# Block 3's gate projections made ahead in plain fp32, three instead of five traces multiplied on GpSimd, and the two lanes of blocks 1 to 7 side by side

## The chip, the cores and the metric

The kernel runs on one core of one Trainium2 chip. The metric is the device time of one execution in microseconds (us), and a run's time is a little longer than the span of its profile, which goes from the first to the last instruction. Engines are called as in the profile: PE is TensorE, DVE VectorE, ACT ScalarE, POOL GpSimd, SP SyncE (here it only issues DMAs).

## What is computed

The input x is 16 sequences of 256 positions with 256 features. Four layers follow one another, each added to its input; the middle two need the whole of what came before, so nothing of a token's layer 3 can start before its layers 1 and 2 are done.

```
ctx      = scan(x, tau_ctx)                                  # h = alpha*h + x_t along the sequence
wg       = sigmoid([x, ctx] @ Wg.T + bg);  gated = x * wg    # the gate projection
mod      = 0.5 + sigmoid(gelu(x @ Wn1.T + bn1) @ Wn2.T + bn2)
temporal = sum_d softmax(blend)_d * scan(gated * mod_d, tau_d)   # 16 traces, d = 0..15
out      = (gelu(x @ Wsoma.T + bsoma) * sigmoid(temporal @ Wtemp.T + btemp)) @ Wout.T
x = x + layernorm(out) * gamma + beta                        # layer 1
x = x + masked attention pooling of x (tanh, exp, one mask of three per sequence)   # layer 2
x = x + (1-sg) * sum_e g_e * (silu(x@Wg_e) * (x@Wu_e)) @ Wd_e + sg * (the same with shared weights)  # layer 3, 8+1 experts
x = x + [gelu(x@W1+b1) @ W2, gelu(x@W1+b1) @ We[index]]      # layer 4
```

## The kernel before, in words

The 16 sequences are 8 blocks (b) of two sequences; the sequences of a block are its lanes (s = 0, 1). Layers 1 and 2 are the side work, cut into 47 pieces for each lane, j = 0 to 46. Layers 3 and 4 are 640 steps: a step takes one chunk of 128 hidden columns of one expert (or of the head, layer 4) for one block.

Of one step, `front` makes the gate and up products on PE, `late` splits the activated product, and `back`, three steps later, makes the down product. PE works with products of three: each fp32 operand is split into a high part of reduced precision (ACT copies) and the rest (DVE subtracts, or POOL for the hidden values), and PE adds low·high, high·low and high·high (`exact_sum`, L641 to L647). `plain_sum` (L634 to L638) multiplies in fp32 unsplit. DVE also multiplies up by the activated gate (`hid`, L1563), and `front(i)` on PE waits for `hid` of step i-2. Chunks of weights come in by SP (`w_raw`, three buffers, L546), are copied high by ACT (L1160) and low by DVE (`w_lo`, L1528); SP fetches the next one when `w_lo` of an earlier one is done.

A side piece of blocks 1 to 7 is: j = 0 the context's scan on DVE (L1303) and the high part of x on ACT, 1 and 2 the high and low halves of x and ctx, 5 the gate projection on PE (`project`, 24 matmuls), 6 gated, 7 to 22 the 16 traces (DVE multiplies and scans, POOL adds, ACT prepares the factor in `mix`), 24 a gather by POOL, 25 to 27 the split of temporal and its projection (`tgate`), 28 to 32 the output projection, 33 to 36 the layer norm (33 a matmul, 34 a reciprocal on DVE that waits for ACT's square root), 38 to 46 the attention.

All engines run the same list of work, written by `order()`. Its first part is block 0's side work alone, the prologue (LEADS, TRACES, TAILS): no step can run before it, and between its pieces stand `pre` parts, unsplit matmuls into `ps_out` that make the soma and the modulation of blocks 1 to 7 ahead, each copied out by ACT, stored to DRAM by SP and read back at block b's piece 2. Each engine keeps the order of the list, so a wait holds up everything behind it on that engine. From there on each step gets as many side pieces as a credit allows (costs in `side_cost`, budget in `step_budget`). Which lane's piece comes next is decided by the cost each has had; LAG gives lane 1 a handicap of 12 cost units, so lane 0 runs some pieces ahead. In the prologue lane 1's multiplications of traces 4, 6, 8, 10 and 12 are done by POOL (`multiply`, L1709) and lane 0's all by DVE (L1403).

Of the kernel before, what the change touches and what calls it, by code (L numbers as in the profile page):

```python
# [43 lines left out]
LAG = 12.0  # L44
# [8 lines left out]
PARTS = [(u, k) for u in range(NPRE) for k in range(3 + u % 2)]  # L53

# [15 lines left out]
HAND = [2, 2, 2, 1]  # L70
# [26 lines left out]
def side_cost(b, j):  # L97

    if 7 <= j < 7 + ND:
        return 2.1  # L100
    return {0: 1.3, 5: 1.0, 34: 1.7, 36: 1.4, 40: 1.4, 42: 1.5, 24: 0.0, 25: 0.0, 29: 0.0, 37: 0.0, 43: 0.0}.get(j, 0.7)
# [11 lines left out]
ON_PE = {2, 3, 4, 5, 27, 31, 33, 38, 40, 41, 44, 46} | set(range(7, 7 + ND))  # L113


def order():
# [8 lines left out]
    for x in LEADS + TRACES + TAILS:  # L125
        if x[0] in (0, 1):
            s, j = x
            out.append(("side", 0, s, j))
            if j < 7 + ND and (s, j) in TRACES + TAILS:
                for _ in range(HAND[slots % len(HAND)]):  # L130
                    if parts:
                        out.append(("pre", *parts.pop(0)))
                slots += 1
            elif s == 0 and 9 <= j < 12:
                out.append(("pre", *parts.pop(0)))
        else:
            out.append(x)
# [143 lines left out]
ON_POOL = (4, 6, 8, 10, 12)  # L281
# [6 lines left out]
           ["gate", "tgate", "proj", "var", "attn", "score", "xT", "probT", "pooled"])  # L288
SIDE_ACT = ((["alpha", "h1", "mod", "mod_hi", "gate0", "gate", "soma", "tgate", "sq", "cen", "std", "attn", "exp", "xT", "probT"],
             ["h1", "mod", "mod_up", "gate", "soma"] + MIXED + ["tgate0", "tgate", "sq0", "sq", "cen", "std", "attn", "exp", "xT", "probT"]),  # L290
            ["x_hi", "ctx_hi", "gate", "alpha"] + MIXED
            + ["t_hi", "tgate", "p_hi", "sq", "cen", "q_hi", "std", "attn", "exp", "xT", "probT"])
# [5 lines left out]
            + ["t_lo", "prod", "p_lo", "q_lo", "rstd", "norm", "affine", "x1", "w_hi", "w_lo", "score",  # L298
               "max", "top", "xT_lo", "den", "rden", "prob", "probT_lo", "res"])
# [3 lines left out]
SIDE_POOL = ((ADDED[:6] + ["xb"] + ADDED[6:], SECOND), ADDED + ["qsum"])  # L303


def stages_in(stages, s, b):

    return stages[1] if b else stages[0][s]
# [14 lines left out]
def residual_stack_kernel(nc, xT, chunks, head_chunks, sidew, vec128, w64, penalties, ident, we_rows,  # L323
# [6 lines left out]
    with ctx:  # L330
# [40 lines left out]
        def row_slot(s, i):  # L371
            if i == 0:
# [15 lines left out]
                   for i in range(2)]  # L388
        pre_soma = [nc.alloc_sbuf_tensor_at(f"pre_soma{i}", [P, DH * S], fp32, offset=at_)
# [89 lines left out]
        s_wide = sem("n1_wide_in")  # L479
        s_back = [sem(f"pre_back{s}") for s in range(BB)]  # L480
# [50 lines left out]
        def _(sp):  # L531
# [53 lines left out]

            load_x(0, 0)
# [17 lines left out]
            for x in ORDER:  # L604
# [28 lines left out]
        def _(pe):  # L633
# [178 lines left out]
            def side(b, s, j):  # L812
# [6 lines left out]
                if j == 5:  # L819
# [49 lines left out]

            def front(i):  # L870
                e, b, c, n = STEPS[i]
                k, slot = n % WSLOTS, b % 2
                if i == 0:
                    pe.wait_ge(pre_act, 2 * NPRE)
# [78 lines left out]
        def _(act):  # L953
# [131 lines left out]
            def side(b, s, j):  # L1085
# [3 lines left out]
                ps, both = ps_side[s], ps_both[s]  # L1089
                if j == 0:  # L1090
# [6 lines left out]
                elif j == 5:  # L1097
                    act.wait_ge(l_pe[s], pe_at(s, b, "gate"))
                    for h in range(DH):
                        last = activate(gated[s][:, h, :], both[:, h, :], ACT.Tanh, bias=half128[:, h:h + 1], scale=0.5)  # L1100
# [116 lines left out]

            def late(i):
# [38 lines left out]
        def _(dve):  # L1257
# [186 lines left out]
            def side(b, s, j):  # L1444
# [9 lines left out]
                if j == 0:  # L1454
# [10 lines left out]
                elif j == 6:  # L1465
                    dve.wait_ge(l_act[s], act_at(s, b, "gate"))
# [368 lines left out]
```

## Time and profile before

| | us |
|---|---|
| median of 3 runs (lowest, highest) | 2795.62 (2795.40, 2796.21) |
| the profiled execution | 2793.71 |
| its span | 2791.1 |
| PE busy in it | 2751.5 (99%) |
| DVE, ACT, POOL busy | 1795.5 (64%), 1450.1 (52%), 1234.8 (44%) |

A timeline row gives start, duration, engine, line, operation, output and inputs, shape, a count where equal neighbours are merged, and in brackets how long the engine was idle before it and what ended that. A plain fp32 matmul stands as two records, so x8 there is four matmuls of the code. Matmuls are pipelined: their pitch is read from starts, not from durations.

### The profile page before, as it was taken

The numbers are of one execution on the slowest core, as the hardware profiler recorded it, in microseconds if no ns is written. First come the engines' busy times: TensorE is split into PE (matmuls) and PEld (weight loads), VectorE is DVE, ScalarE is ACT, GpSimd is POOL, SyncE is SP. The second block draws the span as 40 slices with busy tenths as digits, with TensorE's granted clock in tenths as the row PEclk, the third lists the DMA queues.
The fourth block names the chain that finished last, engine by engine and source line by source line (L and its number), as shares of the span: only waits on it lengthen the run. The fifth ranks groups of instructions, "written<-read, shape, count | busy, mean of one in ns | idle before, by whom it ended". The sixth has DMA issues, their size and how long they took to land.

```text
span 2791.1 us, 36643 instructions
## 1 busy us (share of the span) xinstructions
PE 2751.5 (99%) x12730; PEld 2290.2 (82%) x12730; DVE 1795.5 (64%) x2994; ACT 1450.1 (52%) x2640; POOL 1234.8 (44%) x978
## 2 busy tenths in 40 slices
PE   7899999999999999999999999999999999999999
PEld 6678888888878888888888888888888888888888
DVE  8798778777876666557756766556765563333443
ACT  4655656565447544555545644454644463333445
POOL 7266435533654355434544445433454433333334
PEclk9999999999999999999999999999999999999999
DMA  5344333433223322122322332211321131111232
GB/s 184 108 139 123 98 108 115 132 96 107 80 61 107 94 68 68 55 61 78 98 63 57 90 92 74 59 52 57 109 84 57 43 103 46 46 46 46 80 89 59
DMA packets 119896, 232.68 MB, mean 83 GB/s; under 512 B 13849, under 2 KB 61473, under 8 KB 119713
## 3 DMA queue, kind: packets, MB, share of 16 engines
q1 hardware_dynamic: 84432, 192.46, 22.9%
q10 hardware_dynamic: 32688, 29.47, 4.6%
q0 software_dynamic: 2592, 8.41, 0.9%
q8 instruction: 102, 1.67, 0.3%
q14 instruction: 82, 0.66, 0.1%
HBM read 222.18 MB, written 8.11 MB: 83 GB/s over the span
## 4 chain that ended last, share of the span: by engine, by line
PE 93%; DVE 3%; ACT 1%; issue 1%; SPq 1%; DMA 1%; POOL 0%; ACTq 0%; DVEq 0%; POOLq 0%
PE bank L645 20%; PE bank L646 20%; PE bank L647 20%; PE ps_out L645 10%; PE ps_out L647 10%; PE ps_out L646 10%; PE bank L638 1%; DVE trace L1303 1%; DVE w_lo L1528 1%; DVE trace L1403 1%; DMA mod_rows<-stat 0%; PE bank L683 0%; SPq L550 0%; DVE hid L1563 0%; DVE trace L1477 0%
## 5 line engine op out<-in xcount | busy, mean ns | idle before, releaser
L1728 POOL TENSOR_TENSOR hid_lo<-hid,hid_hi 128x512 fp32r<-128x512 f32 x640 | 854.5, 1335 | 1485.0 <-ACT hid_hi L1231 1484.8
L645 PE MATMUL bank<-res_lo,w_hi 128*128 128x512 f32 x2428 | 952.4, 392 | 5.7 <-DVE hid L1563 4.0
L646 PE MATMUL bank<-res_hi,w_lo 128*128 128x512 f32 x2428 | 946.5, 390 | 0.0
L647 PE MATMUL bank<-res_hi,w_hi 128*128 128x512 f32 x2428 | 944.9, 389 | 0.0
L1563 DVE TENSOR_TENSOR hid<-hid,bank 128x512 f32<-128x512 f32 x576 | 394.1, 684 | 601.1 <-PE bank L647 570.9
L1199 ACT ACTIVATE hid<-bank 128x512 f32<-128x512 f32 x576 | 344.2, 597 | 587.4 <-PE bank L647 584.6
L1528 DVE TENSOR_TENSOR w_lo<-w_raw,w_hi 128x768 fp32r<-128x768 f32 (+2 forms) x520 | 496.7, 957 | 190.1 <-ACT w_hi L1160 142.1
L1160 ACT ACTIVATE w_hi<-w_raw 128x768 fp32r<-128x768 f32 x392 | 331.3, 845 | 489.6 <-PE ps_out L647 472.4
L645 PEld LDWEIGHTS bank<-res_lo,w_hi 128*128 128x128 f32 x2428 | 456.1, 188 | 98.5 <-DVE w_lo L1528 6.1
L647 PEld LDWEIGHTS bank<-res_hi,w_hi 128*128 128x128 f32 x2428 | 455.8, 188 | 96.8
L646 PEld LDWEIGHTS bank<-res_hi,w_lo 128*128 128x128 f32 x2428 | 456.2, 188 | 88.5
L645 PE MATMUL ps_out<-hid_lo,w_hi 128*128 128x512 f32 (+1 forms) x1344 | 509.7, 379 | 2.2 <-DVE acc L1586 2.0
L647 PE MATMUL ps_out<-hid_hi,w_hi 128*128 128x512 f32 (+1 forms) x1344 | 509.7, 379 | 0.0
L646 PE MATMUL ps_out<-hid_hi,w_lo 128*128 128x512 f32 (+1 forms) x1344 | 509.3, 379 | 0.0
L1231 ACT ACTIVATE hid_hi<-hid 128x512 fp32r<-128x512 f32 x640 | 398.8, 623 | 14.6 <-DVE hid L1563 13.8
L1696 POOL TENSOR_TENSOR temporal<-temporal,trace 128x512 f32<-128x512 f32 x239 | 324.3, 1358 | 11.6 <-DVE trace L1303 11.2
L1303 DVE TENSOR_TENSOR_SCAN trace<-bank,trace 128x256 f32<-128x256 f32 x480 | 304.3, 676 | 10.8 <-POOL trace L1709 2.8
L645 PEld LDWEIGHTS ps_out<-hid_lo,w_hi 128*128 128x128 f32 x1344 | 252.5, 188 | 54.9 <-issue 3.2
L646 PEld LDWEIGHTS ps_out<-hid_hi,w_lo 128*128 128x128 f32 x1344 | 252.5, 188 | 49.3
L647 PEld LDWEIGHTS ps_out<-hid_hi,w_hi 128*128 128x128 f32 x1344 | 252.5, 188 | 47.5
L1477 DVE SCALAR_TENSOR_TENSOR trace<-gated,bl,bank 128x256 f32<-128x256 f32 x448 | 193.2, 472 | 0.2 <-ACT bank L1151 0.2
L1586 DVE SCALAR_TENSOR_TENSOR acc<-ps_out,coef,acc 128x256 f32<-128x256 f32 x288 | 119.3, 476 | 1.8 <-issue 1.8
(238 smaller groups left out, 1592.1 us busy)
## 6 DMA issues: line engine op xcount, KB each, us to landing
w_raw<-in_chunks SPq DMA_DIRECT2D x392, 384.0 KB
mod_on<-mod_rows ACTq DMA_DIRECT2D x154, 128.0 KB, 3.2
w_raw<-in_head_chunks SPq DMA_DIRECT2D x64, 224.0 KB
stat<-mod_rows ACTq DMA_DIRECT2D x70, 128.0 KB
x_in<-in_xT SPq DMA_DIRECT2D x16, 256.0 KB, 3.7
pre_x<-in_xT SPq DMA_DIRECT2D x14, 256.0 KB, 7.0
soma_rows<-pre_soma SPq DMA_DIRECT2D x14, 256.0 KB
soma<-soma_rows SPq DMA_DIRECT2D x14, 256.0 KB, 4.0
```

The costliest lines, as they stand in the source:

```text
L645: mm(out, wh, xl, start=start and i == 0, stop=False, skip_group_check=not lone)
L646: mm(out, wl, xh, start=False, stop=False, skip_group_check=not lone)
L647: last = mm(out, wh, xh, start=False, stop=end, skip_group_check=not lone)
L1160: last = activate(w_hi[k][:], raw[:], ACT.Copy)
L1199: activate(h[:], ps_gate[i % 2][:], ACT.Silu).then_inc(s_act, 1)
L1231: activate(hid_hi[i % DEPTH][:], hid[i % 3][:], ACT.Copy).then_inc(s_hhi, 1)
L1303: return V.tensor_tensor_scan(out, decay.broadcast_to([P, S]), x, 0.0, ALU.mult, ALU.add)
L1477: last = STT(tr[:, h, :], gated[s][:, h, :], bl[:, h, d:d + 1], ps[:, 0:S], ALU.mult, ALU.mult)
L1528: return TT(w_lo[k][:, cols], src, f(w_hi[k][:, cols]), ALU.subtract)
L1563: TT(h[:], h[:], ps_up[i % 2][:], ALU.mult).then_inc(s_hid, 1)
L1696: nc.gpsimd.tensor_tensor(temporal[s][:], temporal[s][:], trace[s][d % 3][:], ALU.add).then_inc(l_pool[s], 1)
L1728: nc.gpsimd.tensor_tensor(hid_lo[i % DEPTH][:], hid[i % 3][:], f(hid_hi[i % DEPTH][:]), ALU.subtract).then_inc(s_hlo, 1)
```

## The change

Four things are changed. (1) Block 3's gate projections leave its side work. They are eight parts (`gate_part`), in the prologue behind the last `pre` part: for each lane x times the x half of Wg, and x times the ctx half, both unsplit. ACT copies each result out, SP stores it, and at block 3's piece 0 SP loads both into `ema` and `temporal`; at piece 2 DVE scans the one and adds the other, which gives the same as projecting the scanned x. Pieces 0, 1 and 5 of block 3 lose the rest of their work. (2) ON_POOL keeps traces 4, 6, 8; traces 10 and 12 of lane 1 are multiplied by DVE in the prologue. (3) HAND: two `pre` or gate parts behind every slot instead of 2, 2, 2, 1. (4) LAG is 0, and in one step no two tail pieces with matmuls (j over 26) may have the same j.

```diff
-LAG = 12.0
+LAG = 0.0
+AHEAD = 3
+GATES = [((AHEAD - 1) * BB + s, k0) for s in range(BB) for k0 in (0, DH)]
+PARTS += [("gate", n, h) for n in range(len(GATES)) for h in range(DH)]
-HAND = [2, 2, 2, 1]
+HAND = [2]
-ON_POOL = (4, 6, 8, 10, 12)
+ON_POOL = (4, 6, 8)
@@ order()
-                touched = set()
+                touched, tails = set(), set()
...
-                    if lane in touched and (j in ON_PE or j == 25):
+                    if lane in touched and (j in ON_PE or j == 25) or j in tails:
                         break
+                    if j > 26 and j in ON_PE:
+                        tails.add(j)
@@ SP
+            def gate_store(n, h):
+                if h == DH - 1:
+                    sp.wait_ge(gate_act, n + 1)
+                    for i in range(DH):
+                        sp.dma_start(gate_rows[n, :, i, :], gate_out[n % 2][i][:]).then_inc(s_gstore[n % 2], 16)
+            def gate_back(s):
+                sp.wait_ge(l_dve[s], dve_at(s, AHEAD - 1, "res"))
+                for i in range(2):
+                    sp.wait_ge(s_gstore[i], 16 * DH * len(GATES) // 2)
+                sp.dma_start(ema[s][:], gate_rows[BB * s + 1]).then_inc(s_gback[s], 16)
+                sp.dma_start(temporal[s][:], gate_rows[BB * s]).then_inc(s_gback[s], 16)
@@ PE
-                if j == 5:
+                if j == 5 and b == AHEAD:
+                    return
+                elif j == 5:
+            def gate_part(n, h):
+                u, k0 = GATES[n]
+                if n == 0 and h == 0:
+                    pe.wait_ge(pre_act, pre_at(NPRE - 1, "h1"))
+                elif h == 0:
+                    pe.wait_ge(gate_act, n)
+                last = plain_sum(ps_out[:, 1, h * S:(h + 1) * S], plain(wg, h, pre_x[u % len(pre_x)], k0))
+                if h == DH - 1:
+                    last.then_inc(gate_pe, 1)
@@ ACT
+            def gate_part(n, h):
+                if h < DH - 1:
+                    return
+                act.wait_ge(gate_pe, n + 1)
+                if n >= 2:
+                    act.wait_ge(s_gstore[n % 2], 16 * DH * (n // 2))
+                for i in range(DH):
+                    last = activate(gate_out[n % 2][i][:], ps_out[:, 1, i * S:(i + 1) * S], ACT.Copy)
+                last.then_inc(gate_act, 1)
@@ DVE side
+                if b == AHEAD and j < 3:
+                    if j == 2:
+                        dve.wait_ge(s_gback[s], 32)
+                        for h in range(DH):
+                            last = scan(cen[:, h, :], alpha[:, ND:ND + 1], cen[:, h, :])
+                        last.then_inc(l_dve[s], 1)
+                        mine("ctx")
+                        TT(cen[:], cen[:], temporal[s][:], ALU.add).then_inc(l_dve[s], 1)
```

The first place is PE late in the prologue, from lane 0's `tgate` (bank4<-temporal0) to lane 1's (bank5 and bank1<-temporal1). Before:

```order
77 L638 MATMUL bank4<-temporal0,acc1 128x256 x4
78 L638 MATMUL ps_out<-pre_x2_53,acc1 128x256 x2
79 L638 MATMUL ps_out<-pre_x3_54,n1_wide0_61 128x256
80 L638 MATMUL ps_out<-pre_x3_54,n1_wide1_62 128x256
81 L638 MATMUL ps_out<-pre_x3_54,acc1 128x256 x2
82 L638 MATMUL bank4<-trace0_0,acc2 128x256 x4
83 L638 MATMUL ps_out<-pre_x3_54,acc1 128x256 x2
84 L868 MATMUL bank3<-pre_small0_70,c64 128x256
85 L638 MATMUL bank0<-gated0,mean_w 128x256 x2
86 L950 MATMUL ps_out<-onehot,hid2 128x16
87 L638 MATMUL bank5<-temporal1,acc1 128x256 x2
```

After, on the same engine at the same place:

```order
83 L684 MATMUL bank4<-temporal0,acc1 128x256 x4
84 L684 MATMUL ps_out<-pre_x4_55,acc0 128x256 x8
85 L684 MATMUL bank4<-trace0_0,acc2 128x256 x4
86 L684 MATMUL ps_out<-pre_x5_56,acc0 128x256 x4
87 L684 MATMUL bank0<-gated0,mean_w 128x256 x2
88 L1012 MATMUL ps_out<-onehot,hid2 128x16
89 L684 MATMUL ps_out<-pre_x5_56,acc0 128x256 x4
90 L684 MATMUL bank5<-temporal1,acc1 128x256 x2
```

The soma and modulation parts that stood here have moved ahead of the first row, and the 16 gate matmuls (inputs pre_x4, pre_x5, weights acc0) stand in their place: eight before lane 0's output projection, four before its variance, four before lane 1's `tgate`.

The second place is DVE at the start of block 3. acc1<-bank5,temporal1 is the last piece of block 2's lane 1. Before, block 3's lane 0 had begun earlier and lane 1 starts here:

```order
652 L1520 TENSOR_TENSOR acc1<-bank5,temporal1 128x2x256
653 L1528 TENSOR_TENSOR w_lo1<-w_raw1,w_hi1 128x768
654 L1554 TENSOR_TENSOR res_lo0<-acc1,res_hi0 128x1024
655 L1563 TENSOR_TENSOR hid2<-hid2,bank3 128x512
656 L1303 SCALAR_TENSOR_TENSOR ema1<-alpha,x_in1_1 128x256 x2
657 L1477 SCALAR_TENSOR_TENSOR trace0_1<-gated0,bl,bank4 128x256 x2
658 L1303 SCALAR_TENSOR_TENSOR trace0_1<-bank4,trace0_1 128x256 x2
659 L1528 TENSOR_TENSOR w_lo2<-w_raw2,w_hi2 128x768
660 L1563 TENSOR_TENSOR hid0<-hid0,bank2 128x512
```

After:

```order
644 L1614 TENSOR_TENSOR acc1<-bank5,temporal1 128x2x256
645 L1622 TENSOR_TENSOR w_lo2<-w_raw2,w_hi2 128x768
646 L1648 TENSOR_TENSOR res_lo0<-acc1,res_hi0 128x1024
647 L1657 TENSOR_TENSOR hid0<-hid0,bank2 128x512
648 L1387 SCALAR_TENSOR_TENSOR ema0<-alpha,ema0 128x256 x2
649 L1545 TENSOR_TENSOR ema0<-ema0,temporal0 128x512
650 L1387 SCALAR_TENSOR_TENSOR ema1<-alpha,ema1 128x256 x2
651 L1545 TENSOR_TENSOR ema1<-ema1,temporal1 128x512
652 L1622 TENSOR_TENSOR w_lo3<-w_raw0,w_hi3 128x768
653 L1657 TENSOR_TENSOR hid1<-hid1,bank3 128x512
```

Both lanes now start in one step, rows 648 and 650 wait for the loads of `gate_rows`, and behind them stand a `w_lo` and the next step's `hid`. On SP the two lanes' loads, with block 4's loads of x between them, stand behind a `w_raw` that waits for row 645.

The third place is ACT at the high part of block 1's temporal in lane 1 (one_hi1<-temporal1), the input of that lane's `tgate`. Before:

```order
332 L1231 ACTIVATE hid_hi1<-hid1 128x512
333 L1160 ACTIVATE w_hi8<-w_raw2 128x768
334 L1006 ACT_TABLE_LOAD
335 L1006 ACTIVATE trace0_1,den0<-trace0_0,top0 128x256 x2
336 L1010 ACTIVATE one_hi0<-bank4 128x512
337 L1136 DMA mod_on1_0<-mod_rows 128x256
338 L1136 DMA mod_on1_1<-mod_rows 128x256
339 L1110 ACTIVATE one_hi1<-temporal1 128x512
340 L1199 ACT_TABLE_LOAD
```

After:

```order
326 L1313 ACTIVATE hid_hi0<-hid0 128x512
327 L1231 ACTIVATE w_hi7<-w_raw1 128x768
328 L1204 DMA mod_on1_0<-mod_rows 128x256
329 L1204 DMA mod_on1_1<-mod_rows 128x256
330 L1178 ACTIVATE one_hi1<-temporal1 128x512
331 L1182 ACTIVATE trace0_0<-bank4,half128 128x256 x2
332 L1270 ACTIVATE hid2<-bank1 128x512
```

Lane 0's exponentials with their table load stood before that copy; now lane 0 is at its own `tgate` there and its exponentials come many steps later.

## Rows read from the trace of the kernel before

**Rows 1.** The page: span, and busy time of each engine.
```profile
span 2791.1 us, 36643 instructions
PE 2751.5 (99%) x12730; PEld 2290.2 (82%) x12730; DVE 1795.5 (64%) x2994; ACT 1450.1 (52%) x2640; POOL 1234.8 (44%) x978
```
**Rows 2.** Stretches: PE, PEld, DVE, ACT, POOL busy, clock, DMA share, GB/s.
```profile
0.00:70.00 70.00, 55.56 (x239) 43.30 (x240) 60.71 (x129) 30.78 (x76) 49.36 (x75) 1.00 0.57 183
70.00:140.00 70.00, 59.73 (x261) 46.94 (x260) 52.78 (x89) 43.41 (x84) 19.62 (x17) 0.95 0.37 110
...
1200.00:1400.00 200.00, 200.00 (x938) 167.59 (x937) 138.97 (x240) 104.51 (x200) 92.32 (x71) 1.00 0.29 84
```
**Rows 3.** Timeline, PE: one gate projection, then two steps' first matmuls.
```profile
160.38 0.39 PE L645 MATMUL bank<-one_lo,side_hi 128*128 128x256 f32 x1 [0.54 <-DVE two_lo L1464]
...
163.32 0.40 PE L645 MATMUL bank<-res_lo,w_hi 128*128 128x512 f32 x1
...
171.51 0.39 PE L645 MATMUL bank<-res_lo,w_hi 128*128 128x512 f32 x1
...
175.59 0.39 PE L645 MATMUL bank<-res_lo,w_hi 128*128 128x512 f32 x1
```
**Rows 4.** Timeline, PE, in the prologue.
```profile
70.76 1.96 PE L638 MATMUL bank<-temporal,acc 128*128 128x256 f32 x8 [0.31 <-issue]
...
77.21 1.99 PE L638 MATMUL bank<-trace,acc 128*128 128x256 f32 x8 [1.39 <-DVE trace L1411]
...
83.40 1.96 PE L638 MATMUL bank<-temporal,acc 128*128 128x256 f32 x8 [1.20 <-DVE trace L1403]
85.20 1.89 PE L638 MATMUL bank<-trace,acc 128*128 128x256 f32 x8
...
101.42 5.66 PE L638 MATMUL bank<-soma,gated 128*128 128x256 f32 x16
```
**Rows 5.** Timeline, DVE, in the prologue.
```profile
70.39 0.84 DVE L1403 SCALAR_TENSOR_TENSOR trace<-gated,bl,bank 128x256 f32<-128x256 f32 x2
...
75.30 1.27 DVE L1303 TENSOR_TENSOR_SCAN trace<-bank,trace 128x256 f32<-128x256 f32 x2 [2.76 <-POOL trace L1709]
...
82.24 0.23 DVE L1300 TENSOR_SCALAR bias_b<-ps_out,v 128x16 f32<-128x16 f32 x1 [0.93 <-PE ps_out L950]
```
**Rows 6.** Timeline, POOL, in the prologue: lane 1's trace 12.
```profile
73.87 1.40 POOL L1709 TENSOR_TENSOR trace<-gated,weighed 128x256 f32<-128x256 f32 x2
```
**Rows 7.** Timelines of ACT, PE and DVE around waits of PE.
```profile
318.39 0.62 ACT L1110 ACTIVATE one_hi<-temporal 128x512 fp32r<-128x512 f32 x1
...
319.79 0.39 PE L645 MATMUL bank<-one_lo,side_hi 128*128 128x256 f32 x1 [0.57 <-DVE one_lo L1485]
...
820.78 1.75 DVE L1498 RECIPROCAL stat<-stat 128x256 f32<-128x256 f32 x1 [3.33 <-ACT stat L1129]
...
827.16 0.50 PE L645 MATMUL bank<-res_lo,w_hi 128*128 128x512 f32 x1 [0.73 <-DVE hid L1563]
...
833.44 1.13 PE L638 MATMUL bank<-temporal,wa 128*128 128x256 f32 x4 [1.91 <-DVE temporal L1508]
```
**Rows 8.** DMA issues: name, count, KB each, median us from issue to landing.
```profile
x_in<-in_xT SPq DMA_DIRECT2D x16, 256.0 KB, 3.7
pre_x<-in_xT SPq DMA_DIRECT2D x14, 256.0 KB, 7.0
```
**Rows 9.** Timeline, DVE, where block 2 ends and lane 1 of block 3 starts.
```profile
677.99 0.95 DVE L1528 TENSOR_TENSOR w_lo<-w_raw,w_hi 128x768 fp32r<-128x768 f32 x1
...
680.39 0.68 DVE L1563 TENSOR_TENSOR hid<-hid,bank 128x512 f32<-128x512 f32 x1
680.99 3.08 DVE L1303 TENSOR_TENSOR_SCAN ema<-alpha,x_in 128x256 f32<-128x256 f32 x2
```
**Rows 10.** Timelines of DVE and POOL beside POOL's gathers.
```profile
145.45 3.65 DVE L1528 TENSOR_TENSOR w_lo<-w_raw,w_hi 128x768 fp32r<-128x768 f32 x1
...
146.97 1.31 POOL L1728 TENSOR_TENSOR hid_lo<-hid,hid_hi 128x512 fp32r<-128x512 f32 x1
```

More of the change, by code:

```diff
@@ L113, with part @@
 ON_PE = {2, 3, 4, 5, 27, 31, 33, 38, 40, 41, 44, 46} | set(range(7, 7 + ND))
+def part(x):
+    return x if x[0] == "gate" else ("pre", *x)
 def order():
@@ L131, in order @@
                     if parts:
-                        out.append(("pre", *parts.pop(0)))
+                        out.append(part(parts.pop(0)))
                 slots += 1
             elif s == 0 and 9 <= j < 12:
-                out.append(("pre", *parts.pop(0)))
+                out.append(part(parts.pop(0)))
         else:
@@ L287 @@
             + ["tgate0", "tgate", "proj0", "proj", "var", "attn", "score", "xT", "probT", "pooled0", "pooled"]),
-           ["gate", "tgate", "proj", "var", "attn", "score", "xT", "probT", "pooled"])
+           ["gate", "tgate", "proj", "var", "attn", "score", "xT", "probT", "pooled"],
+           ["tgate", "proj", "var", "attn", "score", "xT", "probT", "pooled"])
 SIDE_ACT = ((["alpha", "h1", "mod", "mod_hi", "gate0", "gate", "soma", "tgate", "sq", "cen", "std", "attn", "exp", "xT", "probT"],
@@ L291 @@
             ["x_hi", "ctx_hi", "gate", "alpha"] + MIXED
+            + ["t_hi", "tgate", "p_hi", "sq", "cen", "q_hi", "std", "attn", "exp", "xT", "probT"],
+            ["gate", "alpha"] + MIXED
             + ["t_hi", "tgate", "p_hi", "sq", "cen", "q_hi", "std", "attn", "exp", "xT", "probT"])
@@ L302 @@
           (["xb"] if d == 7 else []) + [f"add{d}"] + ([f"mul{d + 2}"] if d + 2 in ON_POOL else [])]
-SIDE_POOL = ((ADDED[:6] + ["xb"] + ADDED[6:], SECOND), ADDED + ["qsum"])
+SIDE_POOL = ((ADDED[:6] + ["xb"] + ADDED[6:], SECOND), ADDED + ["qsum"], ADDED + ["qsum"])
 def stages_in(stages, s, b):
-    return stages[1] if b else stages[0][s]
+    if b == 0:
+        return stages[0][s]
+    return stages[2 if b == AHEAD else 1]
 def at(stages, s, b, name):
@@ L388, in residual_stack_kernel @@
                    for i in range(2)]
+        gate_out = [[nc.alloc_sbuf_tensor_at(f"gate_out{i}_{h}", [P, S], fp32, offset=spare[6 + 2 * i + h]) for h in range(DH)]
+                    for i in range(2)]
+        gate_rows = nc.dram_tensor("gate_rows", (len(GATES), P, DH, S), fp32, kind="Internal").ap()
         pre_soma = [nc.alloc_sbuf_tensor_at(f"pre_soma{i}", [P, DH * S], fp32, offset=at_)
@@ L479, in residual_stack_kernel @@
         s_wide = sem("n1_wide_in")
+        gate_pe, gate_act = sem("gate_ahead_pe"), sem("gate_ahead_act")
+        s_gstore = [sem(f"gate_ahead_out{i}") for i in range(2)]
+        s_gback = [sem(f"gate_ahead_back{s}") for s in range(BB)]
         s_back = [sem(f"pre_back{s}") for s in range(BB)]
@@ L610, in _ @@
                     pre_back(x[1], x[2])
+                elif x[0] == "gate":
+                    gate_store(*x[1:])
                 elif x[0] == "side" and x[3] == 0 and x[1] + 1 < NBLK:
                     _, b, s, _ = x
+                    if b == AHEAD:
+                        gate_back(s)
                     if b:
@@ L941, in _ @@
                     pre(*x[1:])
+                elif x[0] == "gate":
+                    gate_part(*x[1:])
                 elif x[0] == "front":
@@ L1089, in side @@
                 ps, both = ps_side[s], ps_both[s]
+                if b == AHEAD and j < 2:
+                    return
                 if j == 0:
@@ L1097, in side @@
                 elif j == 5:
-                    act.wait_ge(l_pe[s], pe_at(s, b, "gate"))
+                    if b == AHEAD:
+                        act.wait_ge(l_dve[s], dve_at(s, b, "gate_in"))
+                    else:
+                        act.wait_ge(l_pe[s], pe_at(s, b, "gate"))
                     for h in range(DH):
-                        last = activate(gated[s][:, h, :], both[:, h, :], ACT.Tanh, bias=half128[:, h:h + 1], scale=0.5)
+                        last = activate(gated[s][:, h, :], (ema[s] if b == AHEAD else both)[:, h, :], ACT.Tanh,
+                                        bias=half128[:, h:h + 1], scale=0.5)
                     last.then_inc(l_act[s], 1)
@@ L1156, in cut @@
                 act.wait_ge(s_raw[n % NRAW], 16 * (n // NRAW + 1))
+                if n == EARLY:
+                    for i in range(2):
+                        act.wait_ge(s_gstore[i], 16 * DH * len(GATES) // 2)
                 if cut_after(n) is not None:
@@ L1242, in _ @@
                     pre(*x[1:])
+                elif x[0] == "gate":
+                    gate_part(*x[1:])
                 elif x[0] == "setup":
@@ L1465, in side @@
                 elif j == 6:
+                    if b == AHEAD:
+                        dve.wait_ge(s_x[s][b % 2], x_at(b))
                     dve.wait_ge(l_act[s], act_at(s, b, "gate"))
```

9 lines of the change are left out of this document (8 added, 1 removed).

## The prediction

> **What bounds the kernel now.** I read the page first, then a table of stretches, then PE's timeline with its idle times, because one number decides which changes can count at all: PE is busy 2751.5 of 2791.1 us [rows 1], so only 39.6 us of the span are not matmuls. The stretches say where they are: 14.4 us of idle PE in the first 70 us and 10.3 in the next 70, while a stretch in the middle has none in 200 us [rows 2]. So there are two regimes. In the prologue PE is not the bound; DVE is (60.7 of 70 us busy), then a chain of small dependent pieces, and added matmuls can be free. Behind it PE is full: a matmul that goes saves its pitch, and anything else counts only where it makes PE wait. The profiled execution took 2793.7 us, 2.6 more than its span; the median is 1.9 above that. The sum is made against 2793.7, and 1.9 is added at the end.
>
> **Block 3's gate projections leave the full stretch.** One lane's projection is 24 split matmuls. The one in the rows starts at 160.38 and the next step at 163.32: 2.94 us [rows 3]. Two lanes: -5.9 us. The pitch is at full clock, and nothing else waits on PE there, so I take all of it.
>
> **The same work in the prologue.** Added are 16 unsplit matmuls. Four of that kind stand between 83.40 and 85.20, so 0.45 us each [rows 4], 7.2 us together, plus four pairs of ACT copies of about 0.62 us (the copy of as many elements in [rows 7]) with a hand-over before each next part. They stand between lane 0's tgate at 70.76 and lane 1's at 83.40. In those 12.6 us other parts stood before, now moved ahead into slots where PE had idle time. Walked through: tgate ends about 72.6, two parts of 1.8 us with one copy between them end about 77.0, lane 0's output projection starts there instead of at 77.21, the third part and the variance end about 81.4, the fourth at 83.2; lane 1's tgate needs DVE's last multiplication, see below. So cost 0, hidden by the chain DVE to ACT to PE of block 0's tail; if that cover is gone, 7.2 plus the copies. The moved parts also cost ACT and SP nothing that ends later: each slot's DVE work is longer than its PE parts, and lane 0's next factor is on PE more than 5 us before its use.
>
> **Traces 10 and 12 from POOL to DVE.** DVE gets two more pairs of multiplications, 0.88 us each by starts (70.39 to the scan behind it) [rows 5]. It loses the wait of 2.76 us for POOL, whose pair for trace 12 ran only at 73.87 [rows 5, 6]. So DVE reaches lane 0's product about 2.76 - 2 x 0.88 = 1.0 us earlier. Late next are the bias, which waits 0.93 us for PE behind the added parts [rows 5], and then lane 1's tgate behind the fourth gate part: 83.2 instead of 83.40. I take -0.2 us, between -1.0 and +1.5.
>
> The clock belongs here: the eight matmuls at 101.42 took 5.66 us, eight records at full clock 1.89 [rows 4], and the granted clock of the stretch is 0.95 [rows 2], so a piece of it ran at 1.2 GHz, after PE had been idle on and off for some 25 us. That is 1.9 us lost. PE is busier until 83 now, but not in the pieces just before the fall, so I leave it; it may go or double, -1.9 to +1.9.
>
> **The loads of block 3.** This is the added wait. DVE's two context scans now wait for DMAs that SP cannot issue before w_lo in the row behind block 2's last piece is done, and behind them on DVE stand a w_lo and the hid of the next step, for which PE's front two steps later waits. With t = 0 at that step's start on PE and 4.08 us a step [rows 3]: PE has front, back and lane 1's last product, 5.5 us; DVE adds it, makes w_lo until 7.3. SP issues the weights, then every 0.45 us one load: the first at 7.7. One load lands after 3.7 us when alone [rows 8], and the queue moves 183 GB/s at a share of 0.57, so about 320 GB/s when full [rows 2], 0.8 us for 256 KB. Lane 0's pair lands about 13.0, lane 1's, with block 4's x between, about 15.5. DVE needs 1.27 + 0.68 per lane [rows 5, 9], so it is through at 17.5, w_lo at 18.4, hid at 19.1. PE would want it at 17.8, so PE waits 1.3, with the hop to the next engine 1.5; I take 1.8 with part of a longer scan. Bounds: 0, if the loads land as fast as one alone; and +6.7 if they land after 7.0 us, as the ten loads in a row did [rows 8], and both scans take 3.08 as at 680.99 [rows 9].
>
> A row shows why scans are unsure: a w_lo took 3.65 us instead of 0.95 and ended 0.8 us after POOL's run of instructions [rows 9, 10]. The Trainium skill (SBUF — State Buffer, section "SBUF: two separate sides") says that VectorE and GpSimd share one pair of ports, that an instruction with two SBUF inputs or one of GpSimd holds it for its whole length, and that the other blocks. The trace agrees. By that rule the added addition (two SBUF inputs, 0.68) would block too, up to 2.7 more a lane; by the row of 128x512 alone it would not. That speaks against the change.
>
> **Lanes side by side.** Four times a tgate waits 0.57 us because its input's high part stands on ACT behind lane 0's exponentials and their table load (318.39, 319.79) [rows 7]; the new order has no exponentials there: -2.3. At 827 and 833 PE waits 0.73 and 1.91 us [rows 7]: DVE had waited 3.33 us for the square root and then had traces of lane 1 and a split of the block's sum behind it [rows 7]. In the new order both lanes are in the tail at once, and there are no traces between: -2.6. The wait of 0.54 before lane 1's first gate [rows 3] goes too. Together -5.4, at best; at worst none of it stays away.
>
> What comes in place: at the starts of blocks 2 and 4 both lanes' scans and halves fall into one or two steps, some 7 us of DVE work in 5.5 us of PE; DVE may be two steps late before PE notices, so +1.0 (0 to 2 for each start). And tails of both lanes in neighbouring steps will collide at places that I can't name: +1.5 (0 to 5).
>
> **Sum.** -5.9 - 0.2 + 1.8 - 5.4 + 1.0 + 1.5 = -7.2: 2793.7 - 7.2 = 2786.5 for a profiled execution, 2788.4 for the median.
>
> **Rivals.** First, waits only move: the 5.4 come back elsewhere, the starts cost nothing extra. -5.9 - 0.2 + 1.8 = -4.3, 2791.3. For it: PE waits for DVE's hid in most of these, and DVE's work is nearly the same. Against it: the named waits have causes that the new order takes apart.
>
> Second, DVE behind block 3's loads at the upper bound: 6.7 instead of 1.8, -2.3, 2793.3. For it, the 3.08 and the 3.65 [rows 9, 10]. Against it, three DMAs a step at a share of 0.3 leave the queue nearly empty.
>
> Third, slower: two lanes starting together. At each of the six later starts DVE has 2 x (3.08 + 0.68 + 0.68) + 0.95 + 0.68 = 10.5 us where PE has two steps, 8.2; if it enters without slack, PE waits 2.3 to 3 us at the scans' users, six times about 16 us: -7.2 + 16 = +8.8, 2804.4. It decides from the point where DVE enters a start more than about 4 us behind. Against it: around 680 DVE made hid, a slow scan, a trace and two w_lo in 10 us, and PE did not wait.
>
> Fourth, the change doesn't do what it says: the unsplit matmuls lengthen the prologue, 7.2 + 4 x 0.62 = 9.7, so +2.5, 2798.1. For it: proj, variance and tgate of block 0 now queue behind them. Against it: the walk above.
>
> **How the numbers follow.** A time within 0.2% (5.6 us) counts as no change. Forecast 0.50 (own range 2785 to 2791.5): 0.46 faster, 0.04 same. Waits only move 0.22: 0.08, 0.13, 0.01 slower. Loads 0.12: 0.03, 0.08, 0.01. Starts 0.08: same 0.02, slower 0.06. Prologue 0.08: 0.01, 0.06, 0.01. Together 0.58, 0.33 and 0.09. The range goes from all waits gone, no wait for the loads and the clock not fallen (-5.9 - 0.2 - 5.4 - 1.9 = -13.4, 2782.2) to 2796.5, which leaves out the third rival and part of the fourth.
>
> **What would show it.** PE's busy time about 1 us higher (5.9 less behind the prologue, 7.2 more in it), its idle time about 8.5 us less (7.2 + 1.3). The first matmul of the steps within 1 us of where it is now. At block 3's start a DVE gap of about 4 us before a scan of ema, ended by a DMA, and one PE wait of 1 to 2 us for hid shortly behind it. No waits for one_lo before tgates. I would be wrong if PE's idle time behind the prologue stays where it was, or if a DMA ends a long gap on DVE there and PE's wait is over 4 us.

## The result and the profile after

The changed kernel takes 2780.74 us (median of 5 runs, 2780.48 to 2782.51) against 2795.40 (2794.57 to 2796.21): a ratio of 0.9948, with a 95% interval of 0.9937 to 0.9959. That is 14.7 us faster. The prediction was 2788.4, 7.2 us faster, with a range from 2782.2: the direction was right, the size was half of it, and the time lies 1.5 us outside the range.

The profiled execution took 2780.48 us, 13.2 less than the one before; the other 1.4 us of the medians' distance is that the profiled execution before was 1.7 us faster than its median, the one after only 0.3. That 1.4 fits TensorE's clock: the profiled execution before had a mean granted clock of 0.999, and of before's 63 executions beside the experiments the four at 0.999 took 2793.1 to 2793.9 us, all others, at 0.997 or 0.998, 2794.4 to 2797.2; the changed kernel's five are all at 0.999. Where the clock fell in those executions no trace shows. The page (span and engines), beside [rows 1]:

```profile
span 2778.3 us, 36629 instructions
PE 2749.1 (99%) x12714; PEld 2290.6 (82%) x12714; DVE 1809.7 (65%) x2996; ACT 1450.1 (52%) x2642; POOL 1235.3 (44%) x974
```

The same stretches as in [rows 2]: PE is 4.2 us busier in the first and 1.9 in the second, and the granted clock of the second is 0.98 where it was 0.95.

```profile
0.00:70.00 70.00, 59.71 (x258) 47.09 (x258) 60.85 (x129) 31.03 (x76) 48.02 (x73) 1.00 0.59 192
70.00:140.00 70.00, 61.61 (x288) 49.87 (x289) 56.28 (x90) 45.86 (x90) 18.08 (x14) 0.98 0.39 122
```

What decides is behind the prologue. These lines say what PE waited for from 112 us to the end: us in total, how many times, the longest. First the kernel before:

```profile
PE bank L645 <- DVE hid L1563: 4.0, 4, 1.5
PE bank L645 <- DVE one_lo L1485: 2.3, 4, 0.6
PE ps_out L645 <- DVE acc L1586: 2.0, 2, 1.7
PE bank L638 <- DVE temporal L1508: 1.9, 1, 1.9
PE bank L645 <- ACT hid L1197: 1.7, 2, 1.5
PE bank L645 <- DVE two_lo L1464: 0.5, 1, 0.5
PE bank L645 <- DVE two_lo L1492: 0.2, 1, 0.2
PE ps_out L645 <- POOL hid_lo L1728: 0.2, 1, 0.2
```

Then the changed kernel:

```profile
PE bank L691 <- DVE hid L1657: 4.1, 3, 1.5
PE ps_out L691 <- DVE acc L1680: 3.2, 3, 1.4
PE bank L684 <- DVE temporal L1602: 0.8, 1, 0.8
PE ps_out L691 <- POOL hid_lo L1822: 0.2, 1, 0.2
```

16 waits of 12.8 us have become 8 of 8.3. Only one of them stands in both, the 1.52 us at the third step. From the first matmul of the steps to the last of the program PE needs 11.7 us less: 5.9 are the 48 gate matmuls, 4.5 these waits, and the remaining 1.3 fit eight waits fewer at 0.16 each: a wait costs that much more than the list says (at 319.79 of before it says 0.57, but the two matmuls' starts stand 0.73 farther apart than in pairs without a wait). The first matmul of the steps itself comes 1.1 us earlier, 106.43 for 107.56.

### The profile page after: what moved, and what is told of

Read it like the earlier page. It is cut to its first block, busy times and chain, and to the rows that moved or that the text cites. A ratio compares the mean times of both kernels' runs of the same rounds, so it can differ in the third digit from the quotient of the medians.

```text
span 2778.3 us, 36629 instructions
## 1 busy us (share of the span) xinstructions
PE 2749.1 (99%) x12714; PEld 2290.6 (82%) x12714; DVE 1809.7 (65%) x2996; ACT 1450.1 (52%) x2642; POOL 1235.3 (44%) x974
## 4 chain that ended last, share of the span: by engine, by line
PE 93%; DVE 3%; ACT 1%; issue 1%; SPq 1%; DMA 1%; DVEq 0%; ACTq 0%
PE bank L691 20%; PE bank L692 20%; PE bank L693 20%; PE ps_out L691 10%; PE ps_out L693 10%; PE ps_out L692 10%; PE bank L684 1%; DVE trace L1387 1%; DVE w_lo L1622 1%; DVE trace L1487 0%; DMA mod_rows<-stat 0%; PE ps_out L684 0%; PE bank L729 0%; SPq L577 0%; DMA temporal<-gate_rows 0%
## 5 line engine op out<-in xcount | busy, mean ns | idle before, releaser
L1622 DVE TENSOR_TENSOR w_lo<-w_raw,w_hi 128x768 fp32r<-128x768 f32 (+2 forms) x520 | 489.0, 942 | 183.0 <-ACT w_hi L1231 142.8
```

The costliest lines, as they stand in the source:

```text
L1622: return TT(w_lo[k][:, cols], src, f(w_hi[k][:, cols]), ALU.subtract)
```

## Experiments

The waits in the table are the sums of that list, from 112 us on. The start is the first matmul of the steps in the one profiled execution.

| kernel | median us (lowest, highest) | ratio to before (95%) | PE waits us (count) | start us |
|---|---|---|---|---|
| before | 2795.40 (2794.57, 2796.21) | | 12.8 (16) | 107.56 |
| changed | 2780.74 (2780.48, 2782.51) | 0.9948 (0.9937, 0.9959) | 8.3 (8) | 106.43 |
| e1_lanes | 2786.79 (2784.35, 2787.53) | 0.9968 (0.9956, 0.9980) | 7.0 (7) | 105.62 |
| e2_gates | 2790.69 (2787.95, 2792.80) | 0.9980 (0.9971, 0.9989) | 14.8 (17) | 108.91 |
| e3_pool | 2782.88 (2781.39, 2783.01) | 0.9953 (0.9939, 0.9966) | 8.2 (8) | 107.21 |
| e4_notails | 2793.82 (2790.09, 2797.15) | 0.9992 (0.9983, 1.0001) | 15.5 (10) | 108.37 |
| e5_tails_old_lag | 2794.25 (2792.08, 2796.68) | 0.9997 (0.9988, 1.0006) | 12.5 (16) | 106.49 |
| e6_space | 2780.86 (2779.36, 2781.99) | 0.9947 (0.9933, 0.9961) | 7.0 (7) | 109.46 |
| e7_no_side_in_head | 2787.75 (2786.45, 2788.64) | 0.9973 (0.9962, 0.9983) | 12.3 (11) | 107.78 |
| e8_fill | 2780.74 (2780.24, 2781.44) | 0.9949 (0.9935, 0.9962) | 8.1 (8) | 106.36 |
| e9_lag2 | 2783.57 (2782.89, 2785.59) | 0.9957 (0.9941, 0.9974) | 9.2 (12) | 109.51 |
| e10_lag4 | 2784.14 (2783.26, 2786.24) | 0.9962 (0.9948, 0.9976) | 9.7 (9) | 106.92 |
| e11_lag6 | 2790.50 (2787.28, 2792.24) | 0.9982 (0.9972, 0.9991) | 13.7 (15) | 106.70 |
| e12_space_fill | 2779.39 (2778.37, 2780.58) | 0.9942 (0.9929, 0.9956) | 7.0 (7) | 106.68 |

**e1_lanes, the order alone.** The kernel before with

```diff
-LAG = 12.0
+LAG = 0.0
...
+                    if lane in touched and (j in ON_PE or j == 25) or j in tails:
                         break
+                    if j > 26 and j in ON_PE:
+                        tails.add(j)
```

> The kernel before with LAG 0 and the rule for tail pieces; no gate projections ahead, five traces on POOL. Theory O (the waits that the prediction left standing, at 149.84, 155.33, 484.48 and 2260 to 2267, went because of the new order of the lanes): PE waits behind the prologue fall by about 6 us, 2789 to 2790. Theory G (they went because block 3's pieces 0 to 5 are gone, which gives DVE and ACT less to do): only the waits that the prediction named go, with new ones for them, 2792 to 2795. Theory C (each new order deals the waits anew): anything between 2786 and 2797, with waits at other places than in the changed kernel. All three: the eight matmuls at the end of the prologue take 5.7 us as before.

It took 9.05 us off (2795.84, the median of before beside these four kernels, to 2786.79), and its list of waits is the changed kernel's without the one at the loads:

```profile
PE ps_out L647 <- DVE acc L1588: 3.2, 3, 1.4
PE bank L647 <- DVE hid L1565: 2.8, 2, 1.5
PE bank L640 <- DVE temporal L1510: 0.8, 1, 0.8
PE ps_out L647 <- POOL hid_lo L1730: 0.2, 1, 0.2
```

Theory O: the waits near 150, 484 and 2265 go with the order of the lanes, not with block 3's pieces. They also stand where the changed kernel has them (465.46, 875.35, 1322.35, 2209.12 and 2249.52 for 466.25, 871.89, 1318.88, 2205.59 and 2245.99): with the new order of the lanes the waits keep their places in both kernels, so theory C, which had them at other places, is wrong too. The time was missed: 2786.79 lies 2.2 us below theory O's range. O counted 6 us of waits alone; in the trace the steps also start 1.9 us earlier than in before, and there are nine waits fewer at 0.16 each beside their length. The end of the prologue was not as all three expected: with the code of before the eight matmuls at 101.11 took 3.72 us, at a granted clock of 1.00, and not 5.66.

```profile
101.11 3.72 PE L640 MATMUL bank<-soma,gated 128*128 128x256 f32 x16
105.62 0.47 PE L905 MATMUL bank<-res_hi,w_lo 128*128 128x512 f32 x1 [0.80 <-ACT res_hi L1183]
```

**e2_gates, the other half.** The changed kernel with `LAG = 12.0` and without the rule.

> The changed kernel with LAG 12 and without the rule for tail pieces: gate projections ahead, HAND and three traces on POOL stay. Theory O: -5.9 (48 matmuls) - 1.1 (clock in the prologue) + 1.3 (loads, less if the lanes start apart) = about -6, 2789 to 2790, with waits for one_lo before three tgates and for hid near 484 and 2265 as before. Theory G: these late waits are gone, 2783 to 2785. Theory C: 2784 to 2794. All: the prologue and its clock are the changed kernel's.

5.15 us off (2795.84 to 2790.69), and all the waits of before are there, at places moved by 2.4 us at most, with one more of 1.45 us at the loads (693.99). Theory O again, 0.7 us above its range; G would have needed 2783 to 2785. The prologue was not the changed kernel's, as all three expected: its code is, but the clock fell near 71 us too, and the steps start at 108.91. The two halves add up: 9.05 + 5.15 = 14.2 of 14.7. This half holds parts (1) to (3) of the change together; HAND, part (3), has no run of its own.

**e3_pool.** The changed kernel with `ON_POOL = (4, 6, 8, 10, 12)`.

> The changed kernel with traces 10 and 12 of lane 1 multiplied by POOL again. By the prediction's walk DVE waits about 1 us longer for POOL, and lane 1's product comes later: +0.5 to +1.2, 2781 to 2782. Rival: the gate parts end at 83.5 and cover it, so no difference (within 0.3 us).

2782.88, 2.1 above the changed kernel, but the intervals of the ratios overlap by most of their width. The waits behind the prologue are the same. In the times it is not resolved. In the trace, from lane 0's `tgate` to lane 1's takes 13.11 us for 12.83 in the changed kernel: 0.28 for the two traces, less than the 0.5 to 1.2 expected and just within the 0.3 of its rival.

**e4_notails.** The changed kernel without the two lines of the rule; LAG stays 0.

> The changed kernel without the rule that no two tail pieces of the same j stand in one step; LAG 0 stays. Theory O: tails of both lanes in one step add PE waits of 0.5 to 2 us at several block ends, 2784 to 2788. Rival (the rule does little, LAG does it): 2780 to 2782. Theory C: 2778 to 2788 with waits at other places.

2793.82: the rule is worth 13 us where LAG is 0, more than any theory gave it. In the profiled execution, the slowest of the eleven (2797.15), PE's waits sum to 7.2 us more than in the changed kernel, and 7.8 are lost in falls of the clock behind them (last section). PE's waits, in the same view:

```profile
PE bank L689 <- DVE hid L1655: 6.4, 5, 3.3
PE bank L727 <- DVE trace L1427: 6.0, 3, 2.2
PE ps_out L689 <- DVE acc L1678: 3.1, 2, 2.2
```

The second row is what the rule forbids: at three block ends both lanes' transposes of the probabilities (piece 44) stand in one step. Lane 0's run at 374.47, and lane 1's follow them at once, while DVE has only just begun lane 1's sums, divisions and normed probabilities. PE, and DVE below it:

```profile
374.47 0.60 PE L727 MATMUL bank<-idn,trace 128*128 128x128 f32 x4
377.05 0.66 PE L727 MATMUL bank<-idn,trace 128*128 128x128 f32 x4 [1.98 <-DVE trace L1427]
```

```profile
373.86 0.68 DVE L1419 TENSOR_TENSOR one_lo<-bank,one_hi 128x512 fp32r<-128x512 f32 x1
...
375.17 0.17 DVE L1424 RECIPROCAL den<-den 128x2 f32<-128x2 f32 x1
375.37 1.63 DVE L1427 TENSOR_SCALAR trace<-trace,den 128x256 f32<-128x256 f32 x2
```

In the changed kernel the two stand at 372.53 and 377.07, more than a step apart, and neither waits. The longest wait, 3.28 us at 699.94, is at block 3's loads: lane 1's stand there behind another `w_lo`, and DVE idles 5.30 us for them, so the rule also shortens that one. The three waits for the probabilities (1.98, 1.88 and 2.17 us) and this one each stand at a fall of the granted clock; the wait of 2.23 us at 474.17 does not.

**e5_tails_old_lag.** The kernel before with the rule alone, LAG 12.

> The kernel before with the rule for tail pieces alone; LAG stays 12. Theory P (the rule only matters where LAG 0 brings both lanes' tails together; the gain is from LAG 0 and the rule together): the waits stand where they stood before, at 149.84, 155.33, 319.79, 484.48, 827, 833 and 2260 to 2267, and the time is that of before within 1 us. Rival T (the rule is the gain whatever the lag): waits fall by about 6 us, 2787 to 2790.

Theory P: the waits stand where they stood (12.5 us, same 16), and the time is within the noise of before. Neither half of part (4) of the change works alone: LAG 0 without the rule is 3.1 us slower than LAG 12 without it (e4_notails against e2_gates), the rule without LAG 0 finds nothing to part.

**e9_lag2, e10_lag4, e11_lag6: how close the lanes must be.** e6_space (next) with `LAG = 2.0`, `4.0`, `6.0`. Their expectations speak of stalls: all distances between starts of neighbouring PE matmuls behind the prologue, less the median distance of the like pair, summed up.

> The kernel with piece 2 of block 3 three steps behind (e6_space), LAG 2 in place of 0: lane 1's pieces stand about two steps behind lane 0's in place of one. In e6_space PE's stalls behind the prologue sum to 16.5 us, in e2_gates (LAG 12) to 26.1, 24.5 without the one at the loads. Theory S (side by side is what takes the waits away, the closer the fewer): between 16.5 and 19 us, 2780 to 2783. Theory D (LAG 0 is one deal among many, and what counts is only that tails don't meet in a step): no trend, 14 to 24 us, some waits at new places.

> As e9_lag2 with LAG 4 (about four steps behind). Theory S: 18 to 21 us of stalls, 2781 to 2785. Theory D: 14 to 24 us without order among LAG 0, 2, 4 and 6.

> As e9_lag2 with LAG 6 (about seven steps behind). Theory S: 20 to 23 us of stalls, 2783 to 2787. Theory D: 14 to 24 us without order among LAG 0, 2, 4 and 6.

The stalls are 16.5 (LAG 0), 19.4, 20.3 and 25.9 us (LAG 6), against 24.5 at LAG 12; the waits of the list 7.0, 9.2, 9.7, 13.7 and 13.3 (14.8 less 1.5 at the loads). LAG 2 is 0.4 above theory S's bound, LAG 4 inside, LAG 6 beyond it and beyond theory D's. But 3.2 us of LAG 6's stalls were lost in two falls of the clock, the only ones behind the prologue in these five traces; without them it has 22.7, inside S's bounds. The times of LAG 2 and LAG 6 (2783.57 and 2790.50) lie 0.6 and 3.5 above S's. The distances were not those expected either: lane 1's transposes stand 3 to 5 us behind lane 0's at LAG 0, 10 to 21 at LAG 2, 19 to 30 at LAG 4, 33 to 47 at LAG 6 and 59 to 78 at LAG 12, where a step is 4.08. So what can be said is: the farther apart the lanes, the more PE stalls. It isn't one lucky order, though five points are no law, and each of them by itself theory D would allow.

**e6_space: the loads.**

```diff
+                    if x == AHEAD and j == 0:  loaded = i
+                    if x == AHEAD and j == 2 and i < loaded + 3:  break
```

> The changed kernel with piece 2 of block 3 at least three steps behind its piece 0, so that the loads land before DVE comes to them. If the loads alone make PE's wait of 1.30 us at 685.66, it goes and the time falls by 1 to 1.5 us: 2779 to 2780. Rival (the scans and additions of both lanes in a row make it, with or without the loads): the wait stays or moves, 2780.5 to 2782.

PE's wait at the loads is gone (8.3 to 7.0 us in the list), and the scan on DVE waits for no DMA; its rows are in the next section. From the first matmul of the steps to the last of the program PE takes 1.5 us less than in the changed kernel. The time is the changed kernel's, because 1.5 us is less than what the prologue scatters: here it ended 3.0 us later. The mechanism is shown by the trace, the gain in time is not.

**e7_no_side_in_head.** e6_space with `and e != HEAD` in the condition of the loop that places side pieces.

> As the kernel with piece 2 of block 3 three steps behind, and with no side pieces in the steps of the head (layer 4). By the reading of the changed kernel's waits (466.25, 871.89, 1318.88 and 2245.99 stand in a head's first steps, where DVE has a trace or a norm beside four w_lo of the head), these go: -4 to -5 us more, 2775 to 2777. Rival: the pieces pushed into other steps make waits there, 2779 to 2784.

My reading of the waits that are left led to a worse order: 2787.75. Of the four named, those at 466.25, 1318.88 and 2245.99 did go and the one at 871.89 became shorter (0.79), but the pieces pushed together elsewhere made new ones, 4.6 us in three waits for `two_lo` alone.

**e8_fill and e12_space_fill: the clock at the end of the prologue.** The changed kernel with 20 extra matmuls (identity by identity, into a bank that nobody reads then) before PE's pieces of block 0's attention, and e6_space with 15.

```diff
+FILL = {(0, 39): 8, (1, 38): 2, (0, 44): 4, (1, 44): 6}      # e12: 5, 2, 4, 4
...
+                for _ in range(n):
+                    mm(ps_out[:, 1, 0:P], f(idn[:]), f(idn[:]), start=True, stop=True)
...
+                fill(FILL.get((s, j), 0))
```

> The changed kernel with 20 extra matmuls on PE in the gaps of block 0's attention (from 91 to 100 us), into a bank that nobody reads there. If what scatters the runs is TensorE's clock falling to 1.2 GHz at the end of the prologue after idle PE, the clock stays at 2.4 GHz there, the steps start at 105 to 105.6 instead of 106.43, and the time falls by 1 to 2 us with less scatter: 2779 to 2780. Rival: the extra matmuls only stand in the way of the chain, +0.3 to +1 us; or the clock falls as before, no change.

> e6_space with 15 extra matmuls in the gaps of block 0's attention, five fewer than in e8_fill, where 16 records of them took 1.79 us in a gap of 1.48. If the two add up (PE's stall of 1.5 us at block 3's start gone, the clock not fallen at the end of the prologue, the chain not delayed), the steps start at about 106 and the time falls to 2778.5 to 2780. Rival: the clock falls earlier in the prologue (near 71 us, as in e6_space) or the same total comes out within the scatter of the runs, 2780 to 2781.5.

In both profiled executions the clock stays at 2.4 GHz: e8_fill has 1.00 from 96 to 102 us, where the changed kernel has 0.76. One such prologue could be luck, as e1_lanes has one without extra matmuls; but over the whole execution seven of the ten executions of these two kernels have a granted clock of 1.000, and none of the ten of the changed kernel and e6_space.

```profile
96.00:102.00 6.00, 4.82 (x38) 3.99 (x37) 4.62 (x14) 4.59 (x13) 0.00 (x0) 1.00 0.00 0
```

But in e8_fill the last pieces start at 101.94 for 101.47, and the time is unchanged. The extra matmuls make only 0.1 of these 0.5 us: lane 0's `tgate`, long before them, already stood 0.4 later (71.06 for 70.69). e12_space_fill has the lowest median, 2779.39; its interval (0.9929 to 0.9956) overlaps with the changed kernel's, so that it beats it by 1.3 us is likely and not shown.

## Why the prediction was wrong

**Right: the gate projections.** -5.9 for 48 matmuls; the work on PE behind the prologue is 5.8 us less in e2_gates and in the changed kernel alike (sum of the median distances of all pairs of matmuls).

**Right: the loads.** +1.8, of which 1.5 was the bare wait; measured 1.30. DVE at block 3's start:

```profile
675.15 0.68 DVE L1657 TENSOR_TENSOR hid<-hid,bank 128x512 f32<-128x512 f32 x1
678.79 2.33 DVE L1387 TENSOR_TENSOR_SCAN ema<-alpha,ema 128x256 f32<-128x256 f32 x2 [2.97 <-DMA temporal<-gate_rows]
681.15 0.69 DVE L1545 TENSOR_TENSOR ema<-ema,temporal 128x512 f32<-128x512 f32 x1
682.05 1.27 DVE L1387 TENSOR_TENSOR_SCAN ema<-alpha,ema 128x256 f32<-128x256 f32 x2 [0.20 <-DMA temporal<-gate_rows]
683.36 0.69 DVE L1545 TENSOR_TENSOR ema<-ema,temporal 128x512 f32<-128x512 f32 x1
683.97 0.95 DVE L1622 TENSOR_TENSOR w_lo<-w_raw,w_hi 128x768 fp32r<-128x768 f32 x1
684.84 0.68 DVE L1657 TENSOR_TENSOR hid<-hid,bank 128x512 f32<-128x512 f32 x1
```

and PE behind that `hid`:

```profile
685.66 0.47 PE L691 MATMUL bank<-res_lo,w_hi 128*128 128x512 f32 x1 [1.30 <-DVE hid L1657]
```

A gap of 2.97 us (about 4 forecast), one scan longer than alone (2.33, POOL ran from 678.79 to 680.57), the chain as walked, and a single wait. The additions took 0.69 with POOL idle. In e6_space, where POOL's `hid_lo` ran from 689.95 to 691.28, lane 1's took 1.60 and ended 0.5 us after POOL:

```profile
688.32 0.69 DVE L1549 TENSOR_TENSOR ema<-ema,temporal 128x512 f32<-128x512 f32 x1
...
690.23 1.60 DVE L1549 TENSOR_TENSOR ema<-ema,temporal 128x512 f32<-128x512 f32 x1
```

The rule weighed in the prediction (the Trainium skill, SBUF — State Buffer, section "SBUF: two separate sides") says that such an addition and GpSimd block each other; this row agrees, at 0.9 us and not the 2.7 that I allowed.

**In part open: the prologue.** The walk came out: lane 0's projection at 76.96 (77.0 forecast), lane 1's `tgate` at 83.52 (83.2), the last pieces at 101.47 for 101.42. So -0.2 was 0.05. That the steps start 1.1 us earlier is the clock: those last matmuls took 4.17 us in place of 5.66 [rows 4].

```profile
76.96 1.89 PE L684 MATMUL bank<-trace,acc 128*128 128x256 f32 x8
...
83.52 1.89 PE L684 MATMUL bank<-temporal,acc 128*128 128x256 f32 x8
...
101.47 4.17 PE L684 MATMUL bank<-soma,gated 128*128 128x256 f32 x16
106.43 0.47 PE L963 MATMUL bank<-res_hi,w_lo 128*128 128x512 f32 x1 [0.80 <-ACT res_hi L1252]
```

The runs say not to read anything into that 1.1: with the prologue of before (before, e1, e5) the steps start at 105.62 to 107.56, with that of the change (changed, e2, e4, e6, e7, e9, e10, e11) at 106.43 to 109.51. The -1.9 to +1.9 of the prediction was no bad bound.

One part of this scatter the traces do settle. From lane 0's `tgate` to lane 1's takes 12.64 us in before and e1, and 12.83 in the changed prologue where the clock stays up there (changed, e7, e8, e10, e11, e12): 0.2 more, where 0.2 less was forecast. Where the clock fell at 70.7 to 72.2 us (e2, e4, e6, e9) it takes 14.5, for instance in e6_space, where lane 0's `tgate` itself took 3.65 us and lane 1's came at 85.13:

```profile
70.61 3.65 PE L688 MATMUL bank<-temporal,acc 128*128 128x256 f32 x8 [1.10 <-issue]
...
85.13 1.89 PE L688 MATMUL bank<-temporal,acc 128*128 128x256 f32 x8
```

In before PE waited 1.39 and 1.20 us for DVE on this way [rows 4]; in the changed kernel the gate parts fill it, PE has one wait of 0.75 us, and DVE waits 1.60 for PE before the bias. In e5, with the prologue of before, a fall at 68.9 us left lane 1's `tgate` at 83.10. So the cost is hidden, as forecast, only while the clock stays up: with a fall there the changed prologue is 1.7 us longer. How often the clock of before falls there isn't known.

**Wrong: "Together -5.4, at best", and the +1.0 and +1.5 that stand in place of it.** Three terms, net -2.9; e1_lanes measures -5.8 in the list (12.8 to 7.0), -7.3 with what each wait costs beside its idle time. By parts:
- The waits named (four for `one_lo`, those at 827.16 and 833.44, and the one before lane 1's gate) all went: 5.5 us, as said.
- The waits not named were taken as staying. All but that of the third step went too: 0.58 and 1.12 at 149.84 and 155.33, 1.49 at 484.48, 0.25 at 858.67, 0.32 at 2001.00, 0.25, 0.18 and 1.71 from 2260 to 2267, together 5.9. That is the step that failed. I had listed the waits whose cause I could take apart, and booked the others as if they belonged to the steps. e1_lanes shows that they hang on the order of the lanes; why, the rows show at one place. The two at 150 came of how side pieces fall beside a step's own work, as the named ones did [rows 10]: at POOL's gathers, lane 0's trace additions and lane 1's start (scan of `ema`) stood in the same steps, POOL ran without a pause, and a `w_lo` on DVE took 3.65 us. In the new order both lanes are at their first traces there, which need no addition; DVE has one trace a step and `w_lo` takes 0.93:

```profile
143.14 1.27 DVE L1387 TENSOR_TENSOR_SCAN temporal<-bank,trace 128x256 f32<-128x256 f32 x2
144.33 0.93 DVE L1622 TENSOR_TENSOR w_lo<-w_raw,w_hi 128x768 fp32r<-128x768 f32 x1
145.72 0.69 DVE L1657 TENSOR_TENSOR hid<-hid,bank 128x512 f32<-128x512 f32 x1 [0.46 <-PE bank L693]
146.32 0.87 DVE L1571 SCALAR_TENSOR_TENSOR trace<-gated,bl,bank 128x256 f32<-128x256 f32 x2
```

  That is a reading of one place; that the other unnamed waits have such causes wasn't tested one by one.
- The two lanes starting together cost nothing: no wait stands at the starts of blocks 2 and 4 (+1.0 forecast), and the third rival with it. Collisions at new places cost 5.4 us (+1.5 forecast, and above its 0 to 5): 0.91, 1.38, 0.92 and 0.17 for `acc` and `hid_lo` at heads, 0.78 and 1.26 near the end.

Named and unnamed waits away, new ones in place: -5.5 - 5.9 + 5.4 = -6.0, the -5.8 of the list but for rounding. By the two profiled executions the whole miss is 6.0 us, -13.2 for -7.2. The lanes are 4.5 of it (-7.4 for -2.9, the 11.7 us behind the first step less gates and loads), the start of the steps 0.9 (-1.1 for -0.2), the loads 0.3 (+1.5 with the 0.16, for +1.8); the rest lies mostly outside the span, where 0.5 us went that nobody had forecast.

Had I taken all 11.4 us of waits that the new order touches as dealt anew, the range would have reached farther down: its lower end, 2782.2, was called "all waits gone" and held only the named ones.

The two sums to be seen on the page: PE's idle time fell by 10.4 us (39.6 to 29.2; 8.5 forecast). Its busy time fell by 2.4 where +1 was forecast: 4.9 more in the prologue for 7.2, of which 1.5 are the shorter matmuls at its end, and 7.3 less behind it for 5.9, which is the gates and eight waits fewer at 0.16.

## What to carry to other kernels

When a change reorders work beside a full engine, every wait of that engine in the reordered stretch may go or move, not only those whose cause one can name: sum them all, and let the range reach from none of them to as many again. Here two chains side by side needed both halves: the lanes close together, and never the same dependent piece of both in one step. Read a gain of 1 to 2 us in the list of waits, which repeats from trace to trace, when the runs scatter as much.

## What the runs showed of the hardware

A short wait of PE could cost more than its length, because the granted clock fell behind it. Behind the prologue the clock falls seven times in these traces: four times in e4_notails, twice in e11_lag6, once in e7_no_side_in_head. Each time PE had just waited, or was still waiting, 1.76 to 3.28 us, and the starts of the matmuls that ran at 1.2 GHz stand 1.6 to 1.7 us farther apart in sum than those of like pairs, 2.7 behind the longest wait. In e4_notails that one, 3.28 us until 699.94, stands in these rows by stretch (the clock is third from the right); the other two are e11_lag6 behind its waits of 1.76 us until 470.48 and 1.96 until 2262.78:

```profile
690.00:700.00 10.00, 6.72 (x31) 5.27 (x29) 4.67 (x8) 2.75 (x5) 1.29 (x1) 0.94 0.42 144
700.00:710.00 10.00, 10.00 (x33) 8.00 (x34) 5.74 (x8) 6.49 (x14) 2.75 (x3) 0.72 0.47 150
```

```profile
470.00:476.00 6.00, 5.52 (x22) 4.57 (x23) 5.02 (x5) 1.84 (x4) 5.80 (x5) 0.72 0.46 136
2262.00:2268.00 6.00, 5.22 (x19) 4.36 (x20) 5.30 (x6) 2.84 (x5) 5.05 (x4) 0.72 0.65 201
```

It isn't certain: six waits of 1.76 to 2.23 us, in before (1.91 at 833.44), e2, e4, e5, e7 and e10, were followed by no fall; nor was any shorter one in these traces. The runs scatter with it: the eleven executions of e4_notails go from 2790.1 us at a mean granted clock of 0.999 to 2797.1 at 0.996. The changed kernel, whose longest wait behind the prologue is 1.52 us, has no fall there.

In the prologue the same code met no fall of the clock (e1), one (before) or two (e5). In e6_space one stands near 71 us, after idle times of PE (3.85 us busy of 6), and another, longer, over the last pieces, which take 6.19 us for the 4.17 of the changed kernel. Two stretches, and PE's last pieces:

```profile
66.00:72.00 6.00, 3.85 (x14) 2.66 (x14) 5.93 (x12) 2.28 (x6) 3.52 (x4) 0.89 0.35 92
102.00:108.00 6.00, 5.83 (x16) 4.85 (x17) 2.24 (x4) 4.12 (x7) 0.00 (x0) 0.50 0.20 66
```

```profile
103.08 6.19 PE L688 MATMUL bank<-soma,gated 128*128 128x256 f32 x16
```
